# Turnings one step later in the attention between features, and moved around the base products and the raised rows in the experts

## What is computed

```python
def _L2_xattn_ref(k, q, v):                                   # stage 7: k = v = context, q = x
    scores = jnp.einsum('bcn,bcm->bnm', k, q) / jnp.sqrt(jnp.float32(input_dim))
    attn = jax.nn.softmax(scores, axis=-1)                    # 512 x 512 for each batch
    out = jnp.einsum('bnm,bcm->bcn', attn, v)
...
def _L3_ffn_ref(x, W_base, b_base, W_router, A, B):           # stages 8 and 11; stage 5 chooses otherwise
    logits = x_flat @ W_router.T
    ...                                                       # the two best of 8 experts, weights that sum to 1
    h = jnp.einsum('nd,erd->ner', x_flat, A)
    hw = h * combine[:, :, None]
    expert_out = jnp.einsum('ner,eor->no', hw, B) * SCALING
    out = x_flat @ W_base.T + b_base + expert_out
```

## Time and profile before

| What | Value |
|---|---|
| Median of 3 runs | 2687.32 us (2685.35 to 2690.18) |
| The profiled execution, its own time | 2690.26 us |
| Its span in the trace | 2689.0 us |
| Mean granted clock of TensorE | 0.991 |
| Busy: PE, PEld, DVE, ACT, POOL | 2577.6, 1682.6, 1581.6, 1073.5, 715.2 us |
| Stage 5, 1761.3 to 1817.7: PE busy | 48.07 of 56.4 us |
| Stage 7, 2044.8 to 2133.9: PE busy | 79.01 of 89.1 us |
| Stage 8, 2133.9 to 2190.0: PE busy | 49.06 of 56.1 us |
| Stage 11, 2633.8 to 2689.0: PE busy | 44.45 of 55.2 us |

### The profile page before, as it was taken

The page is one execution under the profiler, slowest core; times in us unless marked ns, Lnnn a source line. Parts: engine busy times, 40 slices in busy tenths (PEclk is TensorE's granted clock), DMA queues, the critical chain, the costliest instruction groups (busy, mean ns, idle before and its releaser), DMA issues.

```text
span 2689.0 us, 39957 instructions
## 1 busy us (share of the span) xinstructions
PE 2577.6 (96%) x15160; PEld 1682.6 (63%) x15160; DVE 1581.6 (59%) x2953; ACT 1073.5 (40%) x3270; POOL 715.2 (27%) x695
## 2 busy tenths in 40 slices
PE   8999999999998899999999999999998889999998
PEld 7855676776665676556676776547774454556664
DVE  3487666766646566776666765454556644334455
ACT  0014444444463455244444444614454312324440
POOL 1046334444212100463334442122120221000002
PEclk9999999999999899999999999999999999999999
DMA  8541001111001100101001110010000020000000
GB/s 180 93 135 45 25 20 40 40 40 36 20 1 40 48 2 2 60 31 36 8 36 40 40 40 16 1 71 33 2 1 29 21 71 28 13 0 25 13 1 32
DMA packets 55359, 94.86 MB, mean 35 GB/s; under 512 B 31456, under 2 KB 40096, under 8 KB 49024
## 3 DMA queue, kind: packets, MB, share of 16 engines
q1 hardware_dynamic: 55168, 92.30, 11.6%
HBM read 83.89 MB, written 8.39 MB: 34 GB/s over the span
## 4 chain that ended last, share of the span: by engine, by line
PE 86%; DVE 8%; ACT 3%; issue 2%; POOL 1%; DMA 0%; DVEq 0%; SPq 0%; POOLq 0%
PE banks L687 13%; PE banks L775 11%; PE banks L759 4%; PE banks L834 4%; PE banks L803 4%; PE banks L668 4%; PE banks L655 3%; PE banks L303 3%; PE banks L2025 3%; PE banks L1974 3%; PE banks L1450 3%; PE banks L2002 2%; PE banks L2309 2%; PE banks L813 2%; PE banks L2041 2%; PE banks L2275 2%
## 5 line engine op out<-in xcount | busy, mean ns | idle before, releaser
L161 POOL TENSOR_TENSOR norm_spread<-norm_mv,const 128x1 f32<-128x1 f32 x96 | 20.9, 218 | 1149.4 <-DVE norm_mv L157 1149.4
L880 ACT ACTIVATE E_x<-S_x,sm_x 128x128 f32<-128x128 f32 x512 | 199.2, 390 | 262.7 <-DVE sm_x L1052 261.2
L1112 POOL TENSOR_TENSOR QT<-QT,const 128x512 f32<-128x512 f32 x128 | 171.2, 1337 | 470.9 <-DVE turned L938 470.9
L687 PE MATMUL banks<-xT,weights 128*128 128x512 f32 x512 | 237.6, 598 | 5.8 <-POOL weights L1107 5.8
L1016 DVE TENSOR_TENSOR x<-banks,x 128x256 f32<-128x256 f32 (+1 forms) x288 | 147.3, 511 | 123.6 <-PE banks L775 119.6
L775 PE MATMUL banks<-weights,OT 128*128 128x256 f32 x768 | 189.4, 379 | 0.0
L1114 POOL TENSOR_TENSOR QT<-QT,turned 128x512 f32<-128x512 f32 x128 | 169.1, 1321 | 10.0
L887 ACT ACTIVATE OT<-banks 128x512 f32<-128x512 f32 x128 | 76.5, 597 | 227.1 <-PE banks L834 227.1
L687 PEld LDWEIGHTS banks<-xT,weights 128*128 128x128 f32 x512 | 95.3, 192 | 114.6 <-issue 106.8
L775 PEld LDWEIGHTS banks<-weights,OT 128*128 128x128 f32 x768 | 141.8, 190 | 38.3 <-DVE x L1016 11.7
L2405 ACT ACTIVATE E_s<-banks,top_s 128x128 f32<-128x128 f32 x512 | 139.3, 383 | 65.6 <-DVE top_s L2502 65.6
(11 more groups left out here) (315 smaller groups left out, 5192.7 us busy)
## 6 DMA issues: line engine op xcount, KB each, us to landing
weights<-in_L_xwq SPq DMA_DIRECT2D x16, 1024.0 KB, 5.0
weights<-in_L_xwo SPq DMA_DIRECT2D x16, 1024.0 KB, 4.8
weights<-in_L_xwk SPq DMA_DIRECT2D x16, 256.0 KB, 5.0
weights<-in_L_xwv SPq DMA_DIRECT2D x16, 256.0 KB, 2.6
weights<-in_L_ffn_W_base SPq DMA_DIRECT2D x3, 1024.0 KB, 5.0
weights<-in_L_xwq SPq DMA_DIRECT2D x4, 768.0 KB, 5.9
weights<-in_L_xwo SPq DMA_DIRECT2D x4, 768.0 KB, 6.7
xT<-in_xT SPq DMA_DIRECT2D x4, 512.0 KB, 10.1
```

What stands on the lines that cost most here:

```text
L687: mm = PE.matmul(to, left[:, k, head], moving, start=name in ("P1", "P2", "P4", "P5") and k == 0, stop=k == 1, skip_group_check=name in (" ...
L880: ins = AC.activation(e[:, j, :], s[:, j, :], ACT.Exp, bias=sm[:, 0, j:j + 1], scale=1.0, accum_out=sm[:, 1, j:j + 1])
L1112: PO.tensor_tensor(four(to), four(to), spread(cos128, 4), ALU.mult).then_inc(*pool_step.one())
```

## The change

In stage 7 the turnings follow the scores by three steps where they followed by two, and everything behind them (copy, mix, addition, scaling, the norm's turn and copy) moves one step later with them; DVE's division stays one step behind the scores. In the experts three things move in PE's list: `base(0)` goes ahead of `before.turn(B - 1)`; of the two norm turns of a round the first goes ahead of the raised rows (in the last round too); and the banks of the base products are numbered anew, so that the wait for the last batch's copy can stand at batch 2. The lists of ACT, DVE and POOL in the experts are unchanged.

```diff
                 def base_bank(b):
-                    return psum[2 + b % 4]
+
+                    return psum[2 + (b + 2) % 4]
...
                             b = 2 * i + c
+                            if b == 2:
+                                PE.wait_ge(*before.here(B - 1))
                             if b >= 4:
                                 PE.wait_ge(*e_sum(b - 3))
...
                     route(0)
+                    base(0)
                     before.turn(B - 1)
-
-                    PE.wait_ge(*before.here(B - 1))
-                    base(0)
                     for i in range(pairs):
                         PE.wait_ge(*e_weighted(2 * i + 2))
+                        if i == 0:
+
+                            PE.wait_ge(*before.here(B - 2))
...
                             base(i + 1)
+
+                        if i and stage != 11:
+                            norm.turn(2 * i - 2)
                         PE.wait_ge(*e_copied(i + 1))
...
                         if i and stage != 11:
-                            for b in (2 * i - 2, 2 * i - 1):
-                                norm.turn(b)
+                            norm.turn(2 * i - 1)
                     if stage != 11:
                         norm.turn(B - 2)
...
-                        if 2 <= step < units + 2:
-                            u = step - 2
+                        if 3 <= step < units + 3:
+                            u = step - 3
                             PE.wait_ge(*f_prob(u + 1))
...
-                        if step >= 4 and (step - 4) % KC == KC - 1:
-                            b = (step - 4) // KC
+                        if step >= 5 and (step - 5) % KC == KC - 1:
+                            b = (step - 5) // KC
                             DV.wait_ge(*f_mix(b + 1))
...
-                        if step >= 8 and step % KC == 0:
-                            norm.scale(step // KC - 2)
+                        if step >= 9 and (step - 9) % KC == 0:
+                            norm.scale((step - 9) // KC)
```

More of the change, by code:

```diff
@@ L1606, in pe_feature @@
                     PE.wait_ge(*here)
-                    for step in range(units + 3):
+                    for step in range(units + 4):
                         if step < units:
@@ L1615, in pe_feature @@
                             PE.matmul(psum[u % 3][:, :], ctx[:, b, rows_of(j)], x[:, b, :], start=True, stop=True).then_inc(*f_score.one())
-                        if step >= 3 and (step - 3) % KC == KC - 1:
-                            b = (step - 3) // KC
+                        if step >= 4 and (step - 4) % KC == KC - 1:
+                            b = (step - 4) // KC
                             PE.wait_ge(*f_pt(KC * (b + 1)))
@@ L1631, in pe_feature @@
                             mm.then_inc(*f_turned.one())
-                        if step >= 9 and (step - 9) % KC == 0:
-                            norm.turn((step - 9) // KC)
+                        if step >= 10 and (step - 10) % KC == 0:
+                            norm.turn((step - 10) // KC)
                 def act_feature():
                     AC.wait_ge(*before.added)
-                    for step in range(units + 3):
+                    for step in range(units + 4):
                         if step < units:
@@ L1650, in act_feature @@
                             AC.activation(PT[b % 2][:, :, rows_of(j)], four(psum[4 + u % 2][:, :]), ACT.Copy).then_inc(*f_pt.one())
-                        if step >= 9 and (step - 9) % KC == 0:
-                            norm.copy((step - 9) // KC)
+                        if step >= 10 and (step - 10) % KC == 0:
+                            norm.copy((step - 10) // KC)
                     norm.copy(B - 1)
@@ L1656, in dve_feature @@
                     DV.wait_ge(*before.added)
-                    for step in range(units + 4):
-                        if step >= 4 and (step - 4) % KC == KC - 1:
-                            b = (step - 4) // KC
+                    for step in range(units + 5):
+                        if step >= 5 and (step - 5) % KC == KC - 1:
+                            b = (step - 5) // KC
                             DV.wait_ge(*f_mix(b + 1))
```

## The result

The changed kernel took 2700.03 us (median of 8 runs, 2695.01 to 2703.75), the kernel before in the same series 2689.65 us (8 runs, 2685.35 to 2692.8). The ratio is 1.0042, with a 95% interval of 1.003 to 1.0055: the change costs 10.4 us between these two medians and 11.3 by the ratio. The median of before was 2687.32 when three runs were known, so 2.3 us of the distance to the forecast lie in the kernel before.

The account below looks back on a forecast made before the run. Stage 7 bound by a VectorE-ScalarE loop, stage 5's head by the routing weights. -1.0 + 1.4 - 0.8 + 0.9 + 0.3 + 7.5 = +8.3 us on 2687.32 gave 2695.6 us; range 2688.5 to 2700.

Parts of the forecast that it names:

- Stage 7: Loop over VectorE and ScalarE holds no turning; mixes stay 10.7 us apart, last two closer: -1.0 us, bounds 0 and -1.7.
- Heads without the clock: Stages 5, 8, 11, route to `hw` transposes: exponential waits behind the last batch's copy; +1.4, -0.8, +0.9 us.
- Rounds without the clock: Stages 5 and 8: time won in rounds is waited away at their end; about 0 and +0.3 us.
- The clock: Half clock behind longer PE waits: 1.5 us at each of three heads and ends of stages 5 and 8, +7.5 us.
- the stretch of 5.1 us: PE's wait ahead of `hw` in stage 5; it or an end's two waits might bring two falls each, 3.4 us more.
- The median of the kernel before: Base of the forecast for the median: 2687.32 us, to which +8.3 us was added.
- the clock holds: Rival: only +0.8 us is left, 2688.1 us; with one to three falls up to 2692.7; chance 0.27.
- The weights are as slow as before: Rival: POOL's additions hold DVE, 7.96 us again in stage 5, about 2 us more in 8 and 11; 2704 us; chance 0.08.
- TensorE is the bound: Rival: each wait taken from TensorE is won, stage 7 giving 7.4 us; 2670.4 us, faster; chance 0.05.
- the reason that the prediction had given for the last round: Stages' ends: PE arrives 2.65 us earlier but waits for DVE to scale batch 4, raised rows queued behind: +0.8 us.

Follow-up runs that it names:

- the filled kernel: Changed kernel with unread identity transposes in PE's long waits, in the heads and at the ends of stages 5 and 8: 1.0007.
- the rounds but the last: Kernel before with the first norm turn ahead of the raised rows only in rounds 1 and 2 of stages 5 and 8: 1.0017.
- the filled rounds: Kernel before with only rounds 1 and 2 of stages 5 and 8 changed, plus 18 unread transposes ahead of each one's last turn: 0.9981.
- the kernel with both mendings: Changed kernel, but first exponential ahead of the last batch's copy and first turn ahead of raised rows in rounds 1 and 2 only: 0.9997.
- the mended order: Changed kernel with exponential ahead of last copy and first turn moved in rounds 1 and 2 only; with its waits filled by unread transposes: 0.998, 2683.16 us.
- the rounds alone: Kernel before with only the order of norm turns and raised rows in stages 5 and 8 changed, last round included: 1.0018.
- the kernel filled in the heads: Changed kernel with unread transposes only in the heads' waits of stages 5, 8 and 11, the ends' waits left empty: 1.0018.

## Why the prediction was nearly right, and what was off

The direction and the mechanism were right: slower, by a clock that falls behind new waits. The time was not: 2700.03 us lies 4.4 us above the 2695.6 forecast and just above the upper end, 2700. The step that failed is the term for the clock, +7.5 us, which was too small; 2.3 us of the miss are the median of the kernel before.

- **Stage 7** (-1.0): -1.02 in the trace, -1.1 by itself. The argument that the loop has no turning in it is shown by the unchanged 10.71 us between mixes; the wait moved to the norm's turn, 0.41 us against some 0.65 forecast.
- **Heads without the clock** (+1.4, -0.8, +0.9): +1.43, -0.80, +0.90. The steps behind them hold singly in stage 5: the first exponential 9.98 us after the route, 3.99 us from the second to `hw` where 3.07 and about 1 were added up. The removal of GpSimd's additions shows the cause of the 7.96 us. That ScalarE's copy is what makes the exponential late is shown by moving it: 1.0029 became 1.0005.
- **Rounds without the clock** (0 in stage 5 and +0.3 in stage 8): the filled kernel has both stretches with the clock held. The last round to the next stage takes 9.25 us there instead of 7.10, and 8.91 instead of 6.75, against 1.95 and 1.93 won: +0.2 in each stage. The waits of 2.50 us for the scaling were forecast as 2.65.
- **The clock** (+7.5): this is the step that failed, by its size. "1.5 us for each of the three heads and for the end of stages 5 and 8" counts five falls at one price. The windows above show six of them in other places: 6.8 us long behind the 5.17 us in stage 5, two at each end, and none in stage 11. The prediction named the doubling at the stretch of 5.1 us and at the ends and kept it as a bound. By experiment the clock is worth 9.4 us, known to 4 us either way, which alone could not tell it from 7.5; the two traces say 10.6. By the trace the heads cost what was forecast, 4.4 of 4.5 us, and the ends, with two falls each, 6.1 where 3.0 were put; by the timed runs it is the heads that cost more (6.5 and 3). That the heads come out at 4.4 is in part luck, three equal falls forecast where there were a double one, a single one and none. With 9.4 the sum is 0.8 + 9.4 = 10.2 us, and on the median of before as it is known now, 2689.65, it gives 2699.9. That this meets the measured time confirms little, since the 9.4 is itself the distance of the changed kernel from the filled one.
- **The median of the kernel before** was taken from three runs; 2.3 us of the miss are that.

The rivals: "the clock holds" was put at 2688.1, +0.8 us; with the waits filled the clock held, and then the same order took +1.9 by the ratio and +0.8 in the trace. So its sum was right and its condition wasn't met. "The weights are as slow as before" fell with the 3.99 us (its sum, 2687.3 + 16, is 2703.3 and not 2704). "TensorE is the bound" fell with stage 7, whose 7.4 us never came, and with the rounds, whose won time turned up as waits.

The expectation that the rounds but the last would win 3 to 4 us failed for the reason that the prediction had given for the last round: PE is early there and VectorE late. What was not reckoned with is that even 2.40 us of waiting can bring the fall.

Open are 2.0 of the 5.1 us of the filled rounds, why `base(0)` of stage 8 falls in the kernel before and not there, and why of two equal waits one is followed by a fall. The length of the wait doesn't settle it: 1.31 and 1.67 us were followed by a fall in three traces, 2.50 in two others by none. Falls may also differ from run to run, which one trace of each kernel can't show. A hint: the profiled execution of the kernel with both mendings took 2681.36 us, the fastest of its runs (median 2686.92), and shows no fall behind its waits of 2.40 us. In the stretch around 890 us, which no edit touches, the half clock lasts 6.8 us in the trace of before and 13.7 in that of the changed kernel.

## What to carry to other kernels

Before an instruction is moved to fill a wait, ask what the instruction behind it releases: `base(0)` filled two waits of 1.9 us together and delayed the turn, the copy and the exponential by 5.4 us (the second exponential of stage 5 comes 10.08 us behind the route instead of 4.67). Time taken out of the busiest engine is not won where another engine ends the stage; it gathers into one longer idle piece, and on TensorE that piece can be paid twice, as idle time and as work at half the clock. Where such a wait can't be removed, unread transposes in it, fewer than it would hold, cost nothing that was measured here and take the second payment away: 1.0042 became 1.0007, and the mended order only then beat the kernel before (0.998).

## What was not expected of the hardware

- Waits of 2.40 to 2.50 us on TensorE, after long full work, were already followed by 3.4 us at half the clock, and so were waits of 1.67 us (two traces, the product behind them 5.36 and 5.37 us instead of 3.74) and one of 1.31 us (8.73 us instead of 7.03).
- No length of wait decided it in these traces: 1.66 and 1.31 us in the kernel before had no fall behind them, and filling them changed nothing (0.9997); 2.50 us in stage 8 of the rounds alone and in stage 5 of the kernel filled in the heads had none (raised rows in 1.88 us); and in one execution 3.15 us in stage 8 had a fall behind it, 3.14 us in stage 11 none.
- The wait of 5.17 us was followed by 6.8 us at half the clock in one piece, of which the first 1.3 us lay in the wait; where the others were followed by a fall, it was 3.4 us at a time, but for 6.8 us behind 2.40 us at the end of stage 8 of the kernel with rounds 1 and 2 alone.
- A VectorE operation on 16 columns took 1.20 us beside GpSimd's additions and 0.18 us without them; a chain of 14 small operations, six of them held, grew from 3.08 to 7.96 us. The reductions and reciprocals of that chain took 0.17 us either way.
